# First attention's scores as one float32r product per head over stacked high and low rows, operand rows filled through DRAM

## What is computed

```python
q, k, v = qkv[0], qkv[1], qkv[2]           # per window and head, 16 channels
attn = jnp.einsum('bqc,bkc->bqk', q * scale, k)
rel_h = jnp.einsum('bhwc,hkc->bhwk', r_q, Rh)
rel_w = jnp.einsum('bhwc,wkc->bhwk', r_q, Rw)
attn = attn + rel_h[..., :, None] + rel_w[..., None, :]
out = softmax(attn) @ v
```

## Time and profile before

| | us |
|---|---|
| three runs | 901.8, 913.68, 901.2 |
| median | 901.8 |
| the profiled execution, span from first to last instruction | 909.1 |
| attention 0 in it, up to the first product of MLP 0 | 389.7 |

### The profile page before, as it was taken

One profiled execution on the slowest core, in us unless ns is written; L12 is line 12 of the kernel. 1 busy time (PEld: TensorE's weight loads), 2 busy tenths in 40 slices (PEclk: granted clock), 3 DMA queues, 4 the chain that ended last, 5 costly groups with the idle time before them and its releaser, 6 DMA issues.

```text
span 909.1 us, 20167 instructions
## 1 busy us (share of the span) xinstructions
PE 828.7 (91%) x6794; PEld 693.4 (76%) x6794; DVE 511.1 (56%) x1514; ACT 434.4 (48%) x1419; POOL 137.4 (15%) x243
## 2 busy tenths in 40 slices
PE   3688899899999988988997999999999999997998
PEld 2576777677767676678996788888888888776998
DVE  3165565666676857455434475757565666464452
ACT  1044353555464645354334465655555555365432
POOL 9110101011010110023122010101101010100211
PEclk9589696999999998599996999999999999799999
DMA  8482010101001010010004122130404030400001
GB/s 123 74 183 41 3 33 2 34 8 28 18 16 27 6 34 1 1 36 1 1 4 67 33 40 44 28 57 16 71 0 69 0 69 1 71 1 1 19 18 35
DMA packets 39904, 29.89 MB, mean 33 GB/s; under 512 B 13336, under 2 KB 37992, under 8 KB 39826
## 3 DMA queue, kind: packets, MB, share of 16 engines
q1 hardware_dynamic: 36488, 26.16, 15.4%
q0 software_dynamic: 2528, 2.35, 1.8%
q10 hardware_dynamic: 810, 0.40, 0.3%
HBM read 8.79 MB, written 1.57 MB: 11 GB/s over the span
## 4 chain that ended last, share of the span: by engine, by line
PE 71%; SPq 15%; DVE 6%; issue 4%; DMA 2%; ACT 1%; POOL 1%; DVEq 0%; POOLq 0%; ACTq 0%
PE bank L1195 10%; PE bank L1274 8%; PE bank L486 7%; PE bank L465 6%; SPq L1103 6%; PE bank L1222 5%; PE bank L895 5%; PE bank L1202 5%; SPq L1122 4%; PE bank L1241 3%; PE bank L912 3%; PE bank L1302 3%; PE bank L1334 3%; SPq L1550 3%; PE bank L1013 2%
## 5 line engine op out<-in xcount | busy, mean ns | idle before, releaser
L655 ACT ACTIVATE Pb<-bank,nmax 128x256 f32<-128x256 f32 (+1 forms) x432 | 192.2, 453 | 105.0 <-DVE nmax L645 100.8
L645 DVE TENSOR_REDUCE nmax<-bank 128x2 f32<-128x392 f32 (+2 forms) x240 | 138.8, 578 | 35.4 <-PE bank L1195 33.2
L666 DVE TENSOR_SCALAR Pb<-Pb,rsum 128x196 f32<-128x196 f32 (+2 forms) x432 | 134.6, 349 | 8.5
L685 ACT COPY area<-bank 98x392 f32<-98x392 f32 (+1 forms) x144 | 77.1, 536 | 106.3 <-PE bank L1202 75.3
L1195 PE MATMUL bank<-K,Q 80*128 80x256 f32 x384 | 109.5, 411 | 6.0 <-DMA Q<-rel_dense 5.6
L895 PE MATMUL bank<-K,Q 80*128 80x196 f32 x384 | 96.5, 380 | 17.3 <-DMA Q<-dense_k 15.6
L1195 PEld LDWEIGHTS bank<-K,Q 80*128 80x128 f32 x384 | 70.4, 201 | 26.4 <-issue 15.0
L895 PEld LDWEIGHTS bank<-K,Q 80*128 80x128 f32 x384 | 72.1, 218 | 21.8 <-issue 14.9
L655 ACT ACTIVATION_READ_ACCUMULATOR Pb<-bank,nmax 128x1 f32 x432 | 87.4, 202 | 0.0
L685 DVE COPY area<-bank 60x128 f32<-60x128 f32 (+2 forms) x96 | 43.4, 452 | 62.6 <-PE bank L915 25.2
L475 ACT ACTIVATE area<-bank,fc1b 128x256 f32<-128x256 f32 x96 | 45.2, 475 | 66.0 <-PE bank L465 65.7
(11 more groups left out here) (141 smaller groups left out, 1516.5 us busy)
## 6 DMA issues: line engine op xcount, KB each, us to landing
Q<-dense_q SPq DMA_DIRECT2D x16, 288.0 KB, 5.0
K<-dense_k SPq DMA_DIRECT2D x16, 288.0 KB, 6.9
Q<-dense_q SPq DMA_DIRECT2D x48, 32.0 KB, 2.0
K<-dense_k SPq DMA_DIRECT2D x48, 32.0 KB, 2.0
Q<-rel_dense SPq DMA_DIRECT2D x32, 48.0 KB, 3.1
Q<-rel_dense POOLq DMA_DIRECT2D x32, 48.0 KB, 2.8
out<-x_all SPq DMA_DIRECT2D x8, 192.0 KB, 2.0
x_all<-in_x SPq DMA_DIRECT2D x1, 1344.0 KB, 9.5
```

Source lines behind the costliest of these rows:

```text
L645: nc.vector.tensor_reduce(nmax[0:sc.shape[0], u % 3, 0:sc.shape[1]], sc, AX.X, ALU.max, negate=True).then_inc(self.m_rdy, 1)
L655: nc.scalar.activation(Pb[u % 3][0:rows, t, 0:cols], sc[:, t, :], ACT.Exp, bias=nmax[0:rows, u % 3, t:t + 1], accum_out=esum[0:rows, u % 3 ...
L666: nc.vector.tensor_scalar(Pb[u % 3][0:rows, t, 0:keep], Pb[u % 3][0:rows, t, 0:keep], rsum[0:rows, u % 3, t:t + 1], None, ALU.mult).then_i ...
L685: copy(*self.pt_views(u)).then_inc(self.pt[self.pt_engine(u)], 1)
```

## The change

- Each value of q, k and rel is split in two: high is the value rounded to float32r, low is what is left, also in float32r. q.k then is high.high + low.high + high.low, and it is computed as one product over stacked rows: Q0 has q high, q low, q high on rows 0 to 47 and rel high (h, w) and rel low (h, w) on rows 48 to 103; K0 has k high, k high, k low and the one-hot pattern twice. Scores are one float32r product per tile. Q0, K0, QR0, KR0 and KP0 take up to 107 of 128 rows and are float32r.
- A remainder unit is four products with 128 columns of weights: QR0 holds each head's queries in its own half of the columns and zeros in the other, so two heads add up in one bank (`start=(j == 0), stop=(j == 1)`).
- ACT and DVE write q and k twice, high and whole. POOL subtracts (`pool_low`). DVE subtracts rel high from the bank for h right behind the copy (slot 6) and for w in slot 8 (`dve_rel_low`).
- SP stores eight whole tiles to DRAM for each image (q, k, rel h and rel w, high and low) and loads ten back as rows (two of them twice). The operands' head 2h + g is head h of channel half g, so that a row's two halves lie together; the projection's weights and v are ordered to match.
- Fourteen constant DMAs instead of seven, eight for the even buffers and six for the odd: the patterns are needed twice. The six are issued by POOL, which waits for them before image 0; c_hot1 too is issued by POOL. The weights of MLP 1 share SBUF with attention 0's operands and are loaded by SP once attention 0 has ended. ACT spreads KP0's rows with two DMAs.

```diff
-K0ROWS = D0 + 2 * WS
+Q0ROWS = 3 * D0
+K0ROWS = Q0ROWS + 2 * (2 * WS)
...
-        early_sizes = {"KP0": HEADS * N0, "QR0_0": HEADS * RPAD, "QR0_1": HEADS * RPAD, "KR0_0": HEADS * NREM,
...
+        early_r_sizes = {"KP0": HEADS * N0, "QR0_0": HEADS * P, "QR0_1": HEADS * P,
...
+        Q0 = [sb(f"Q_{i}", [P, HEADS, T], F32R) for i in range(2)]
+        K0 = [sb(f"K_{i}", [P, HEADS, T], F32R) for i in range(2)]
+        Q1, K1 = [[m[0:K1ROWS].bitcast(F32) for m in ms] for ms in (Q0, K0)]
...
+        stash = {name: [nc.dram_tensor(f"stash_{name}_{i}", (rows, 2 * T), F32, kind="Internal").ap() for i in range(2)]
+                 for name, rows in (("q_high", CH), ("q_low", CH), ("k_high", CH), ("k_low", CH),
+                                    ("h_high", GH0 * WS), ("h_low", GH0 * WS), ("w_high", GH0 * WS), ("w_low", GH0 * WS))}
...
+            hot = Q0ROWS + 2 * WS
+            return [(KR0[i][Q0ROWS:hot], per_head(a["c_hotrem"][0:2 * WS])),
+                    (KR0[i][hot:KR0ROWS], per_head(a["c_hotrem"])),
+                    (windows[:, :, 0, 0:RPAD], per_pair(a["c_qwin"])), (windows[:, :, 1, RPAD:P], per_pair(a["c_qwin"])),
+                    (K0[i][Q0ROWS:hot], per_head(a["c_hot0"])), (K0[i][hot:K0ROWS], per_head(a["c_hot0"]))]
...
+        first_rows = [(KP0[Q0ROWS:Q0ROWS + 2 * WS], per_head(a["c_hotpad"][0:2 * WS])),
+                      (KP0[Q0ROWS + 2 * WS:KR0ROWS], per_head(a["c_hotpad"]))] + constant_rows(0)
...
+                for keys, lo, hi in ((KR0[p], 0, NREM), (KP0, NREM, NREM + N0)):
+                    for j in range(2):
+                        mm = nc.tensor.matmul(S_BANK[u % 3][:, lo:hi], QR0[p][0:KR0ROWS, 2 * h + j, :],
+                                              keys[0:KR0ROWS, 2 * h + j, :], start=(j == 0), stop=(j == 1))
...
+                for dst in (self.q_high[:, g, :].bitcast(F32R), self.qd[:, g, :]):
+                    nc.scalar.activation(dst, G_BANK[0][0:CH, 0:T], ACT.Identity,
+                                         bias=qb0[:, g:g + 1]).then_inc(self.g_out[0], 1)
...
+            def pool_low(self, eng, n):
+                eng.wait_ge(self.g_out[0], n.at(9, 5))
+                nc.gpsimd.tensor_tensor(self.q_low.bitcast(F32R), self.qd, self.q_high, ALU.subtract).then_inc(self.low, 1)
+                eng.wait_ge(self.g_out[1], n.at(8, 5))
+                nc.gpsimd.tensor_tensor(self.k_low.bitcast(F32R), self.kd, self.k_high, ALU.subtract).then_inc(self.low, 1)
...
+                high, src = self.rel_views(1, self.rel_high[0])
+                nc.vector.tensor_copy(high.bitcast(F32R), src).then_inc(self.g_out[1], 1)
+                eng.wait_ge(self.g_out[1], n.at(8, 6))
+                nc.vector.tensor_tensor(self.rel_views(1, self.rel_low[0])[0].bitcast(F32R), src, high,
+                                        ALU.subtract).then_inc(self.g_out[1], 1)
...
+            def dve_rel_low(self, eng, n):
+                eng.wait_ge(self.g_out[0], n.at(9, 6))
+                high, src = self.rel_views(0, self.rel_high[1])
+                nc.vector.tensor_tensor(self.rel_views(0, self.rel_low[1])[0].bitcast(F32R), src, high,
+                                        ALU.subtract).then_inc(self.g_out[0], 1)
...
-            def scatter_rel(self, eng, p, heads):
-                for h in heads:
-                    for i in range(2):
-                        eng.dma_start(Q0[p][D0 + i * WS:D0 + (i + 1) * WS, h:HEADS:GH0, :],
-                                      self.reld[i][h * WS:(h + 1) * WS, :, :]).then_inc(self.relscat, 16)
...
+            def from_stash(self, eng, dst, of, d):
+                return eng.dma_start(dst.rearrange("d (h g) t -> d h (g t)", g=2).bitcast(F32),
+                                     of.rearrange("(h d) x -> d h x", d=d))
...
+                    eng.dma_start(stash["q_high"][p], self.flat(self.q_high)).then_inc(self.stash_high, 16)
+                    eng.wait_ge(self.g_out[1], n.at(8, 5))
+                    land(eng, "sp")
...
+                    eng.wait_ge(self.low, n.at(2, 2))
+                    land(eng, "sp")
+                    eng.dma_start(stash["q_low"][p], self.flat(self.q_low)).then_inc(self.stash_low, 16)
+                    eng.dma_start(stash["k_low"][p], self.flat(self.k_low)).then_inc(self.stash_low, 16)
...
-                    for h in range(GH0):
-                        for src, dst in ((self.qd, Q0), (self.kd, K0)):
-                            eng.dma_start(dst[p][0:D0, h:HEADS:GH0, :], src[h * D0:(h + 1) * D0, :, :]).then_inc(self.scat, 16)
...
+                    for at in (0, 2 * D0):
+                        self.from_stash(eng, Q0[p][at:at + D0], stash["q_high"][p], D0).then_inc(self.scat, 16)
+                    for at in (0, D0):
+                        self.from_stash(eng, K0[p][at:at + D0], stash["k_high"][p], D0).then_inc(self.scat, 16)
+                    eng.wait_ge(self.stash_low, n.at(16 * 2, 16 * 2))
                     land(eng, "sp")
-                    self.scatter_rel(eng, p, range(GH0 // 2) if n.index0() else range(GH0))
+                    self.from_stash(eng, Q0[p][D0:2 * D0], stash["q_low"][p], D0).then_inc(self.scat, 16)
...
+                    eng.wait_ge(self.g_out[1], n.at(8, 7))
+                    land(eng, "sp")
+                    eng.dma_start(stash["h_high"][p], self.flat(self.rel_high[0])).then_inc(self.relstash, 16)
+                    eng.dma_start(stash["h_low"][p], self.flat(self.rel_low[0])).then_inc(self.relstash, 16)
+                    eng.wait_ge(self.g_out[0], n.at(9, 7))
+                    land(eng, "sp")
+                    eng.dma_start(stash["w_high"][p], self.flat(self.rel_high[1])).then_inc(self.relstash, 16)
+                    eng.dma_start(stash["w_low"][p], self.flat(self.rel_low[1])).then_inc(self.relstash, 16)
+                    eng.wait_ge(self.relstash, n.at(16 * 4, 16 * 4))
+                    land(eng, "sp")
+                    for i, name in enumerate(("h_high", "w_high", "h_low", "w_low")):
+                        at = Q0ROWS + i * WS
+                        self.from_stash(eng, Q0[p][at:at + WS], stash[name][p], WS).then_inc(self.relscat, 16)
                 image(Img(0, 0))
                 after_first()
                 image(Img(0, 1))
...
+                self.pool_low(eng, n)
+                eng.wait_ge(self.scat, n.at(16 * 6, 16 * 6))
...
+                for j in range(2):
+                    gather(QR0[p][0:K0ROWS].rearrange("p (h j) q -> p j h q", j=2)[:, j, :, RPAD * j:RPAD * (j + 1)],
+                           Q0[p][0:K0ROWS].rearrange("p (h j) t -> p j h t", j=2)[:, j], self.gath)
...
+        def act_meanwhile(act):
+            act.wait_ge(kpad_done, 2)
+            act.dma_start(KP0[D0:2 * D0].bitcast(F32), KP0[0:D0].bitcast(F32)).then_inc(ld_kpad, 16)
+            act.dma_start(KP0[2 * D0:Q0ROWS].bitcast(F32), kpad_low).then_inc(ld_kpad, 16)
...
-                sp.wait_ge(zeroed_odd, 2)
-                for dst, src in late_odd:
-                    sp.dma_start(dst, src).then_inc(ld_odd, 16)
...
+                pool.wait_ge(zeroed_odd, 2)
+                for dst, src in late_odd:
+                    pool.dma_start(dst, src).then_inc(ld_odd, 16)
...
+                pool.wait_ge(ld_odd, 16 * len(late_odd))
```

204 lines of the change are left out of this document (116 added, 88 removed).

## The result

The changed kernel takes 982.0 us (median of 4 runs, 976.0 to 985.0) against 907.7 (median of 4, 901.2 to 915.5): ratio 1.081, 95% interval 1.073 to 1.088. It is slower by 74 us. The forecast was 887, with a range to 915.

A forecast was written before the change was run, and what follows sets the result against it. The prediction took the first attention's images to wait on SP's DMA queue and DVE, although PE is 91% busy. Sum: 909.1 - 16 (intervals) + 9 (start) - 8 (last image) = 894; at 0.992 for median runs, 887 us, range 862 to 915.

The forecast's parts named there:

- the loads of rel rows: Before each next image's first scores: a 168 KB load onto 14 partitions was taken to land in 3.3 us.
- the start: Up to image 1's first scores: more constants on POOL's queue were to make it 9 us later (0 to 24).
- Float32r ... 0.22 and 0.28 for the remainder: PE time per score unit after the change, in us (main, remainder), freeing PE of 7.3 us an image.
- First scores to slot 8 ... 24.5: First part of each image's interval: DVE's work was to let it shorten by only 1.0 us, 25.5 to 24.5.
- rival 2: With PE idling more, every image may start at 1.2 GHz: six intervals 240 against 245, in runs 898 us; chance 0.2.
- rival 4: The chain behind slot 8 isn't shorter: loads onto 14 rows take 5 us, stores queue; in runs 897 us; chance 0.1.
- POOL's first x gather 47: At the start: POOL, waiting for all its constants, was to issue image 0's first gather at 47 us instead of 40.5.
- 17 us for the whole chain: Image 1's first scores were to come 17 us (20 now) after SP's later weights at 85, so at 102.
- The last image -8: Image 7, run by PE at 1.2 GHz: of 14 us given back, about 8 were to come through (3 to 12).
- rival 1: PE's freed time comes through whole: intervals of 31 us, a total of 847, in runs 840 us; chance 0.1.
- The 10.8 us of the second part: From slot 8 to the next image's first scores: the chain of stores and loads was to take 10.8 against 12.5.
- Rival 3: Constants on POOL's queue end at 112 us and hold image 0; total 959, in runs 951 us; chance 0.17.

The follow-up runs named there:

- e4_twice: The changed kernel with every float32r score product issued twice into the same place; 965.5 us, ratio 1.064.
- e1_f32: The changed kernel with its scores computed as float32 products over the same stacked rows; 960.1 us, ratio 1.059.
- b_half: The kernel before, with main units' products computing only 98 of 196 score columns from image 2 on; 919.9 us, ratio 1.010.
- e13_f32_wide: The changed kernel with float32 score products and rel loads onto 84 partitions, relative-position terms left out of the scores; 935.8 us, ratio 1.032.
- a_split: The changed kernel with its DMAs of 31 constant rows split into 28 and 3 rows; 961.7 us, ratio 1.058.
- e3_wide: The changed kernel with the four rel loads sent onto 84 partitions instead of 14, relative-position terms left out of the scores; 969.6 us, ratio 1.069.
- b_split: The kernel before with each constant DMA of 31 rows issued as one of 28 and one of 3; 900.3 us, ratio 0.992.

## Why the prediction was wrong

Three steps failed: the clock (at nothing in the sum; 18 us over the six intervals), the loads of rel rows (3.3 us taken, 6.7 measured; 23 us), and the start (+9 taken, +36 measured). Point by point, against the profiled executions:

1. **"Float32r ... 0.22 and 0.28 for the remainder": mis-sized.** Measured 0.28 to 0.40 and 0.53 to 0.62 at full clock. I took 118 ns from 256-column products of which 36 follow one another. Two main products here start 185 ns apart at full clock (median; 115 where four follow one another, in e4_twice), and the page's group of their weight loads has its engine busy for 190 ns each at full clock, 333 at half, 278 on average:

```profile
L920 PEld LDWEIGHTS bank<-K,Q 128*128 128x128 f32 x192 | 43.6, 278 | 28.1 <-issue 20.0 <-ACT Pb L680 4.9 <-DMA Q<-stash_w_low 2.1
```

A remainder unit also changed its form: before, the products of its two heads with 64 stationary columns each started 14 ns apart (median), side by side; now each product takes all 128 columns, and they start 112 to 164 ns apart, one behind another. In float32 it takes 1.11 us in e1_f32 against 0.60 before. PE's relief is 12 x 0.3 = 3 to 4 us an image at full clock, not 7.3.

2. **"First scores to slot 8 ... 24.5", and rival 2 on the clock: this is the step that failed most.** Against the forecast the six intervals are 57 us too long, some 36 of them in the first part (27.2 as a mean by my sum, 33.1 measured) and 22 in the second (11.0 and 14.6). I gave the clock 0.2 and priced it at 11 us. It cost 18.0 us in the six intervals (286.7 to 268.7 in e1_f32, net of the float32 work that brings it up), and e4_twice and b_half show the direction with nothing but TensorE's work changed. The error in the price: I assumed that an image at low clock would be like the two of the earlier trace rows, low for some 13 us and then up again. After the change the clock stays at 0.50 for up to 38 us at a stretch, and the mean of 0.67 means two thirds of the six intervals at 1.2 GHz. The Trainium skill ("TensorE: Matmul & The Clock Gate", Why this matters for your kernels) asks for a busy TensorE; cited as a rival, it was the right way to look.

My slot-by-slot sum also had a wait of PE at nothing that the trace shows in every image. POOL's subtraction of k, DVE's scaling of two tiles, and the transposes that wait for it:

```profile
388.62 1.28 POOL L1070 TENSOR_TENSOR dense_k<-dense_k 96x512 fp32r<-96x512 f32 x1
...
388.32 1.69 DVE L691 TENSOR_SCALAR Pb<-Pb,rsum 128x196 f32<-128x196 f32 x2
...
390.07 1.09 PE L937 MATMUL bank<-ident,Pb 128*98 128x128 f32 x4 [2.02 <-DVE Pb L691]
```

The second scaling takes 1.32 us instead of 0.32; in all seven images it starts 0.08 us behind POOL's subtraction and ends 0.12 us behind it. PE waits 2.0 us for it, and each time the clock falls 1.6 to 4.0 us after that wait began (at 103.0, 150.8, 198.6, 246.3, 294.1, 341.9 and 389.7 us) and stays at 0.50 for 17 to 38 us. In e1_f32 the scaling is as long, but PE, with more to do before it, waits 0.9 us and the clock does not fall there; in e4_twice it waits 1.4 us and the clock falls there in four of seven images. So these two runs changed the wait along with the work, and no run moves the subtraction away: how much of the clock that alone would give back stays open. It is not the whole story either: in b_half, which has no such subtraction, the clock falls three times (164.8, 209.2 and 332.1 us) while PE has no wait at all.

3. **"A load of 168 KB onto 14 partitions ... I take 3.3": mis-sized, 6.7.** The bounds in the text (up to 5 in rival 4) did not hold it either. The rest of the chain was right: second w store at 2.85 (2.88 here: 402.27 to 405.15), landed 4.85 (5.1), last load issued at 7.5 (6.5, since SP's issues take 0.4 and not 0.85), POOL's subtractions 1.25 (1.27). In my sum it makes 10.8 + 3.4 - 1.0 = 13.2; in this last interval 13.3 was measured, as a mean 14.6, the clock being low in most. In the runs at full clock the loads cost 22.8 us (e1_f32 to e13_f32_wide). Four loads of 168 KB at the 112 GB/s of their window take 6.1 us: 672 KB at that rate, not one DMA's latency, is what the last of four waits for. The Trainium skill ("SBUF — State Buffer", Door 1: The DMA port swizzle) has DMA bandwidth go by how many of the 16 ports the rows reach, 109 GB/s for rows on four ports. By its table of partitions the 14 rows of a rel load and the 16 of a q or k load reach four, and the windows have 112 and 116: the trace agrees. An estimate by that page, 1.6 us for one load and 6.3 for four, would have shown it beforehand. (The 2 us and 436 GB/s that the prediction took from the Trainium skill's "DMA: Bandwidth & Descriptors", Anatomy of one DMA, are given there for DMAs that POOL issues; the stores here are SP's, so the comparison with 2.0 us says nothing of the receipt.)

4. **"The start ... +9": it was +35.9 at image 1.** Three steps. "POOL's first x gather 47" was 56.4: I added bytes at 236 GB/s, where the queue's pace was set by one engine and small packets. The prediction had even named the case ("31 rows may lie on one engine") and drawn only that the new rows would spread; three DMAs of 31 rows stayed, and a_split takes 21.3 us off image 1's first scores. "From there all is serial: 17 us" was 27.6, with q and k loads of 10 us and rel stores queued behind them (the chain's 10.71). And "17 us for the whole chain" of image 1 behind SP's later weights (done at 97.1, forecast 85) was 31.8, at half clock and over the same loads.

5. **"The last image -8"** was -2.6: the relief per unit at half clock is 0.8 us for a main unit (1.31 to 0.52), as forecast, but 0.1 for a remainder (1.07 to 0.95, forecast 0.64). DVE is busy for 27 us of the 41.9, and the mean clock is 0.64 against 0.70 before. How these share the missing 5 us no run shows.

6. **Right:** DVE's load (30.5 us, forecast 29.3; 1.0 of the difference is the long scaling above); that PE's relief would not come through whole (rival 1), though with the clock down no run tests the reason given, DVE; and that SP had time to spare in the images. The 10.8 us of the second part were met in two intervals of e3_wide, but with loads that the forecast did not have, and not in e13_f32_wide (12.9, with float32 scores); that is no confirmation. Rival 3 had the right place, POOL's constants, but not the size: the gathers started at 56, ahead of the 62 given as the turning point, and the time still went over 2% slower, because the turn was worked out with the six intervals gaining 16 us.

What adds up, in this order of removal: the start +36 (of which 21 by the 31-row DMAs), the clock +18, the narrow loads +23, and -6 elsewhere make 71. In the other order the loads are 10 and the clock 31. What stays open is whether float32r scores would gain anything with the clock held up: the versions that held it did so by spending the time that float32r had freed. Also open is what exactly the clock goes by; e1_f32 and e4_twice have PE busy for 239 and 241 us of their six intervals, at 0.96 and 0.84, and differ in the wait behind POOL's subtraction (0.9 and 1.4 us).

## What to carry to other kernels

When a change takes work off TensorE in a stage that is not purely bound by it, price the stage at the lower clock first; the test is cheap: issue the removed work again as copies, and see whether the time falls. Then look for the wait of PE ahead of each fall of the clock, and for what it waits for. Before you route a tensor through DRAM, look at how many rows each load lands on and at the outermost dimension of each store: total bytes at the narrow rate, not the latency of one DMA, are what the last load waits for. And a DMA over 31 rows is worth splitting into 28 and 3: here that alone took 7 us off the kernel before and 20 off the changed one.

## What the runs showed of the hardware that I had not expected

- The same DRAM rows load at 242 GB/s onto 84 partitions and at 112 onto 14: a narrow destination stretches a 2 KB packet from 84 ns to 260 (medians; 326 onto the 16 rows of q and k).
- A store whose destination is walked as 6 x 14 rows uses six engines (share 0.38) and lands 7.8 us behind its issue, a plain one of the same bytes 2.2.
- Removing half of the main score columns of six images from the kernel before makes it 1% slower; computing every float32r score twice makes the changed one 16 us faster.
- An engine that issues DMAs behind a slow one on its queue stands in the issue itself: POOL 12.9 us, ACT 20.3.
- A DVE instruction of 0.32 us takes 1.32 beside POOL's subtraction of k, ending 0.12 us behind it, in all seven images of the changed kernel (and of six other versions).
- A DMA of 31 rows has one packet in flight (1.01 on average, 62 packets in 21 us); as 28 and 3 rows, 4.6 in flight and 5 us (b_split).
- A casting DMA of 31 rows onto float32r brings some 5,400 packets of 4 bytes with it; split into 28 and 3 rows they are nearly gone.
- Float32r products of 128 stationary and 196 moving columns start 185 ns apart at full clock in pairs, 115 when four follow one another (e4_twice).
